# Four transformer stages on one NeuronCore: a batch loop ahead of the token steps, or a quarter of the next batch in each of them

## The chip, the cores and the metric

One core of one Trainium2 chip runs the whole program. The metric is the device time in microseconds of one execution, as the median of several runs; a profiled execution of the same program gives the trace.

## The reference

The input x is 4 batches of 512 tokens of 512 values. Four residual stages follow each other, each on the layer norm of what came before:

```python
x = x + tanh(g_xattn[0]) * smooth_quant_mlp(ln(x), fside, ctx)     # A: two int8 "SmoothQuant" linears, silu between
x = x + tanh(g_ffn[0])   * bit_ffn(ln(x), gate_w, val_w, out_w)    # B: ternary weights, 512 -> 2048 -> 512
x = x + tanh(g_xattn[1]) * (ln(x) @ attention(ctx).T)              # C: softmax((ctx Wq+bq)(ctx Wk+bk).T), 512 x 512 a batch
x = x + tanh(g_ffn[1])   * moe(ln(x), router_w, down_w, up_w)      # D/E: 8 experts, top 2

def smooth_quant_linear(x, w):
    s = sqrt(max|x| over tokens / max|w| over rows)                # one value a column
    x_q, w_q = round((x / s) / x_scale), round((w * s) / w_scale)  # a scale for each row
    return x_q @ w_q.T * x_scale * w_scale.T
```

Stage A needs all 512 tokens of a batch for its column maxima: its first linear (called h) has a 512 x 512 weight, its second (called o) a 512 x 256 weight, and both weights differ in every batch. Stage C's attention weights depend on the batch's context alone. B, C, D and E work on 128 tokens at a time.

## The kernel before

The instructions of each engine are written out by hand in one program order, and engines meet through counting semaphores. An engine takes its instructions strictly in that order, so one that waits holds everything behind it. There are two blocks.

The first block (L377 to L1306) handles whole batches. `step0` loads the ternary weights of gate and val, rounds and transposes them, and does the first linear of batch 0 and the column maxima of batch 1. Then a hardware loop, `step(b)` for b = 1 and 2 and once more for 3, does the first linear of batch b, the second linear and the attention weights of batch b-1, and the column maxima of batch b+1. The attention weights of all four batches stay in `att_t`. `last_step(3)` does the second linear and attention of batch 3 and, between them, sums, rounds and transposes the out weights (`w_sum`, `w_round`, `w_ternary`, `w_transposed` with m = 2).

The parts of a batch are, on PE: `columns` (fp32 transposes for the column maxima), `rows` (spreads the smoothing factors over the partitions by a product with ones), `integers` (fp16 transposes of the rounded values), `scale_row`, `products`, and for attention `t_context`, `t_query_key`, `t_energies`, `t_transpose`. ACT copies what PE leaves in PSUM, rounds to integers (`rounded`, four activations) and exponentiates. DVE takes maxima, scales and dequantises; POOL takes roots, makes diagonals and scales the weights and the hidden values by rows.

The second block (L1344 to L1692) has 16 token steps of 128 tokens. In step i PE computes four chunks of gate and val (`b_chunk`, L1618 to L1625, each a bias product and four products for each of the two), the output of step i-1 (`b_output`, 16 products on activations that 4 DMA transposes deliver), the transpose and the attention product of step i-1 (`spread` of `ln_c`, `c_attend`), and router, experts and their output of steps i-2 and i-3. A chunk's gate goes through ACT (silu), its val through DVE (product with the silu, then the maximum). `p_gate` and `p_val` have two PSUM banks each, `p_tr` and `p_out` two each. ACT's order in a step is: silu 0, norms, silu 1, `lt_d`, silu 2, `ln_c`, rounding of x, `lt_c`, silu 3, copy of x, four roundings.

## Time and profile before

| | us |
|---|---|
| median of 3 runs (598.85 to 600.71) | 600.53 |
| the profiled execution | 600.03 |
| its span, first to last instruction | 598.2 |
| PE busy in the span | 467.9 |
| DVE busy | 417.7 |
| ACT busy | 332.4 |
| POOL busy | 220.2 |

The mean TensorE clock granted is 0.922 of full speed. Engines: PE is TensorE's matmul, DVE VectorE, ACT ScalarE, POOL GpSimd, SP the engine that issues the DMAs. A timeline row gives start and duration in us, then engine, line, operation, output<-input and count, and in brackets the idle time ahead of it with what ended it. A group row gives total busy time and the mean in ns after the bar.

### The profile page before, as it was taken

Reading aid. Unit: us, or ns where it says so; the run is one execution under the profiler, and the core shown is the slowest. Engines: PE = TensorE matmul, PEld = TensorE weight load, DVE = VectorE, ACT = ScalarE, POOL = GpSimd, SP = SyncE. Lnnn points to the kernel's source line nnn. Section 1 sums busy time; section 2 is a strip of 40 time slices with the busy share of each in tenths; the row PEclk is TensorE's granted clock in tenths of the full one; section 3 lists DMA queues with packets and bytes.
Section 4 is the critical chain, followed back from the end, with each engine's and each line's share of the span. In section 5 each row is a group of like instructions: output and inputs, shape, how many; then the busy total and the mean of one; then the engine's idle time right before and its main releaser. Section 6 shows DMA issues by size and latency. Waiting matters only on the chain.

```text
span 598.2 us, 7373 instructions
## 1 busy us (share of the span) xinstructions
PE 467.9 (78%) x2278; PEld 240.1 (40%) x2310; DVE 417.7 (70%) x983; ACT 332.4 (56%) x543; POOL 220.2 (37%) x343
## 2 busy tenths in 40 slices
PE   0546867857865657689899999999999998999863
PEld 0425544434433334233344444444444444444332
DVE  4678798998994687455576677667766776576541
ACT  2558769829838839654545555555555455554411
POOL 2344255535535345522333333333333342332121
PEclk9865999979978987799999999999999999999995
DMA  8985003021003500010121022102220122022210
GB/s 315 249 334 176 1 5 107 1 70 35 0 1 116 200 1 18 1 35 1 36 37 35 19 53 54 35 21 51 54 51 13 44 54 38 19 50 54 36 38 32
DMA packets 56547, 37.25 MB, mean 62 GB/s; under 512 B 43192, under 2 KB 45496, under 8 KB 56000
## 3 DMA queue, kind: packets, MB, share of 16 engines
q1 hardware_dynamic: 56512, 36.82, 21.5%
q8 instruction: 17, 0.28, 0.2%
q14 instruction: 18, 0.15, 0.1%
HBM read 24.15 MB, written 4.19 MB: 47 GB/s over the span
## 4 chain that ended last, share of the span: by engine, by line
PE 44%; issue 4%; ACT 4%; DMA 3%; SPq 2%; DVE 1%; POOLq 0%; POOL 0%
PE p_gate L1625 9%; PE p_out L1632 8%; PE p_out L1665 7%; PE p_val L1625 7%; DMA p_t<-p 3%; PE p_gate L1622 3%; PE p_tr L1613 3%; PE p_out L1650 2%; PE p_out L1640 2%; ACT ln_c L214 2%; SPq L1356 2%; ACT p L1561 1%; PE p_out L1654 1%; PE p_tr L252 1%; PE p_out L1661 0%
## 5 line engine op out<-in xcount | busy, mean ns | idle before, releaser
L1556 ACT ACTIVATE silu_g<-p_gate,bcol 128x512 f32<-128x512 f32 x64 | 44.0, 687 | 97.3 <-PE p_gate L1625 83.2
L1412 DVE TENSOR_TENSOR u<-p_val,silu_g 128x512 f32<-128x512 f32 x64 | 44.3, 692 | 44.2 <-PE p_val L1625 44.2
L1625 PE MATMUL p_val<-val_t,q_room 128*128 128x512 bf16 x256 | 67.0, 385 | 0.0
L1665 PE MATMUL p_out<-out_t,p_t 128*128 128x512 f16 x256 | 61.0, 385 | 6.3 <-DMA p_t<-p 6.3
L1625 PE MATMUL p_gate<-gate_t,q_room 128*128 128x512 bf16 x232 | 61.6, 384 | 4.0 <-issue 4.0
L1381 POOL TENSOR_TENSOR ey<-e_base,y 128x8 f32<-128x8 f32 x16 | 26.5, 1657 | 99.0 <-DVE y L1452 99.0
L1632 PE MATMUL p_out<-att_t,lt_c 128*128 128x512 f32 x128 | 58.4, 599 | 0.7 <-ACT lt_c L1529 0.7
L164 POOL TENSOR_TENSOR rstd<-mv,ln_eps 128x1 f32<-128x1 f32 x48 | 9.2, 193 | 118.9 <-DVE mv L209 118.8
L1428 DVE SCALAR_TENSOR_TENSOR x_all<-p_out,tanh_g,x_all 128x512 f32<-128x512 f32 x32 | 24.0, 750 | 38.0 <-PE p_out L1632 25.2
L1561 ACT ACTIVATE p<-u,bcol 128x512 f16<-128x512 f32 x64 | 40.9, 709 | 10.3 <-DVE bcol L1422 10.3
L1414 DVE TENSOR_REDUCE mu<-u 128x1 f32<-128x512 f32 x64 | 43.9, 686 | 2.2
L1665 PEld LDWEIGHTS p_out<-out_t,p_t 128*128 128x128 f16 x256 | 23.7, 99 | 41.4 <-DMA p_t<-p 15.2
L1625 PEld LDWEIGHTS p_val<-val_t,q_room 128*128 128x128 bf16 x256 | 25.3, 99 | 30.8 <-issue 1.1
L207 DVE BATCH_NORM_STATS2 stats<-x_all 128x6 f32<-128x512 f32 x48 | 32.7, 681 | 3.4 <-PEq L377 2.0
L920 ACT ACTIVATE q_room<-out_t,qscale 128x512 f16<-128x512 f32 x32 | 20.4, 713 | 24.2 <-DVE qscale L668 24.2
L1632 PEld LDWEIGHTS p_out<-att_t,lt_c 128*128 128x128 f32 x128 | 23.1, 190 | 23.9 <-issue 23.0
L1625 PEld LDWEIGHTS p_gate<-gate_t,q_room 128*128 128x128 bf16 x256 | 19.9, 98 | 30.2 <-issue 15.3
L518 POOL TENSOR_TENSOR x_all<-x_all,o_hs 128x512 f32 (+1 forms) x16 | 20.5, 1306 | 22.3 <-DVE o_hs L677 22.3
L1622 PE MATMUL p_gate<-bias_rows,q_room 9*128 9x512 bf16 x64 | 24.8, 388 | 4.8 <-PEq L377 3.0
L165 POOL TENSOR_TENSOR rstd<-rstd,half_neg 128x1 f32<-128x1 f32 x48 | 26.3, 549 | 3.8
L632 DVE TENSOR_REDUCE colmax<-p_tr 128x1 f32<-128x512 f32 x32 | 20.9, 686 | 8.4 <-PE p_tr L1114 8.4
L1622 PE MATMUL p_val<-bias_rows,q_room 9*128 9x512 bf16 x64 | 24.9, 388 | 0.0
(225 smaller groups left out, 1063.1 us busy)
## 6 DMA issues: line engine op xcount, KB each, us to landing
att_t<-in_L_ffn_gate_w SPq DMA_DIRECT2D x4, 1024.0 KB, 11.4
h_region<-in_fside_BxS2xS SPq DMA_DIRECT2D x4, 1024.0 KB, 5.5
att_t<-in_L_ffn_val_w SPq DMA_DIRECT2D x4, 1024.0 KB, 9.7
out_dram<-x_all SPq DMA_DIRECT2D x16, 256.0 KB, 2.3
h_region<-in_L_ffn_out_w SPq DMA_DIRECT2D x3, 1024.0 KB, 5.6
x_all<-in_x SPq DMA_DIRECT2D x2, 1024.0 KB, 5.6
ctx_sb<-in_ctx SPq DMA_DIRECT2D x4, 512.0 KB, 3.4
x_all<-in_x SPq DMA_DIRECT2D x1, 2048.0 KB, 10.4
```

Of the source, the lines that this page charges most:

```text
L165: link(nc.gpsimd.tensor_tensor(rstd[:, s:s + 1], rstd[:, s:s + 1], half_neg[:, 0:1], ALU.pow))
L207: link(nc.vector.bn_stats(stats[:, s, :], tile_of(n)))
L1381: nc.gpsimd.tensor_tensor(ey[:, :], e_base[:, :], y[:, :], ALU.pow).then_inc(d_exp, 1)
L1412: nc.vector.tensor_tensor(cols, p_val[:, c % 2, :], silu_g[:, c % 2, :], ALU.mult).then_inc(u_done, 1)
L1414: return nc.vector.tensor_reduce(mu4[:, c:c + 1], cols, AX_X, ALU.max, apply_absolute_value=True)
L1428: nc.vector.scalar_tensor_tensor(tile_of(n), p_out[:, bank, :], factor, tile_of(n), ALU.mult, ALU.add).then_inc(done, 1)
L1556: nc.scalar.activation(silu_g[:, c % 2, :], p_gate[:, c % 2, :], ACT.Silu, scale=col(CG)).then_inc(silu_done, 1)
L1561: nc.scalar.activation(p16[:, cols], u[:, cols], ACT.Copy, bias=ROUND16, scale=col(QS)).then_inc(b_p16, 1)
L1622: nc.tensor.matmul(bank[:, c % 2, :], x_t[n % 2][rows, D:AUG], bias_aug[m][:, cols], start=True, stop=False)
L1625: last = nc.tensor.matmul(bank[:, c % 2, :], x_t[n % 2][:, k * P:(k + 1) * P], w_t[m][:, k, cols], start=False, stop=k == KD - 1)
L1632: last = nc.tensor.matmul(p_out[:, 0, :], lt_c[:, k * P:(k + 1) * P], att_t[:, bass.ds((n // T) * (KD * S) + k * S, S)], start=k == 0, sto ...
L1665: last = nc.tensor.matmul(p_out[:, 0, :], p_t[:, k * P:(k + 1) * P], w_t[2][:, k, :], start=False, stop=k == KH - 1)
```

## The change

The two blocks become one and the batch loop goes. Batch 0 is done ahead of the token steps (`weights_and_first_linear`, `first_batch`: the former `step0` and `last_step`, now with b = 0), and so are the column maxima and first scaling of batch 1. The rest of batches 1 to 3 is cut into quarters, one for each token step: `quarter(i)` gives batch and quarter, so that steps 0 to 2 carry quarters 1 to 3 of batch 1, steps 3 to 6 batch 2, steps 7 to 10 batch 3, and step 11 the leftovers. Quarter 0 is the norm of the batch and its column maxima (and the end of the batch before), 1 context, query and key and the first rounding, 2 the first linear with the first two energies, 3 the second linear with the last two.

PSUM is shared anew: gate and val take turns in a ring of three banks, the fourth (`p_sum`) collects the output and the attention product, `p_tr` serves norms, router and experts, and `p_out` is left to the quarters. `att_t` holds two batches. The out weights are loaded behind the bias rows on SP's queue. The norm of batches 2 and 3 goes from DVE to ACT, the softmax scaling in steps from ACT to POOL; DVE reads the smoothing row from PSUM and not from a copy.

```diff
+        ring = [p_gate[:, 0, :], p_gate[:, 1, :], p_val[:, 0, :]]
+        p_sum = p_val[:, 1, :]
...
+        def half(n, c, m):
+            return ring[(2 * (HC * n + c) + m) % 3]
...
+        def quarter(i):
+            b, k = divmod(i + 5, 4)
+            return b, k, b < NB
...
+                    x_load(2)
+                    sp.wait_ge(bias_split, 2)
...
+                                sp.dma_start(bias_aug[m][row:row + 1, :].rearrange("o (p n) -> o p n", p=P),
+                                             bias_part[:, s, col:col + n]).then_inc(aug_loaded, 16)
+                    for c in range(4):
+                        w16_by(sp, 4 + c)
+                        w_load(2, c)
...
+                def first_batch():
+                    t_context(0)
+                    w_sum(2, 1)
+                    t_query_key(0)
+                    o_smooth_rows(0)
+                    t_exponential(0, 0)
...
                 def step(i):
+                    b, k, live = quarter(i)
                     act.wait_ge(q_cols, i + 1)
                     b_gate(i, 0)
                     if i >= 2:
                         d_norm(i - 2)
+                    if k == 0 and 2 <= b <= NB:
+                        t_transposed(b - 1, 2)
+                        t_transposed(b - 1, 3)
+                    if live and k == 0:
+                        h_normalise(b)
+                    if live and k == 1:
+                        t_context(b)
+                    if live and k == 2:
+                        t_exponential(b, 0)
+                        t_exponential(b, 1)
+                        h_rounded(b, 1)
+                    if live and k == 3:
+                        t_transposed(b, 0)
+                        t_transposed(b, 1)
+                        o_smooth_rows(b)
...
                     b_gate(i, 2)
+                    if live and k == 3:
+                        o_rounded(b, 0)
+                        t_exponential(b, 2)
+                        t_exponential(b, 3)
+                    if live and k == 2:
+                        h_silu(b, 0)
                     if i >= 1:
-                        c_norm(i - 1)
+                        c_transposed(i - 1)
                     if i + 1 < NT:
-                        q_scaled(act, i + 1)
-                    if i >= 1:
-                        c_transposed(i - 1)
+                        q_scaled(i + 1)
+                    if live and k == 1:
+                        h_rounded(b, 0)
                     b_gate(i, 3)
...
+                def half_free(j):
+                    if j >= 3:
+                        pe.wait_ge((silu_done, u_done)[(j - 3) % 2], (j - 3) // 2 + 1)
...
+                def d_project(n):
+                    pe.wait_ge(d_lt, n + 1)
+                    if n + 1 < NT - 1:
+                        pe.wait_ge(c_lt, n + 2)
```

ACT's queue, from the third silu of a step to the silu of the tokens in D: before, in any step (`q_room` holds x, `p` the rounded activations, `lt_c` the transposed norm).

```order
L1556 ACTIVATE silu_g<-p_gate,bcol 128x512
L214 ACTIVATE ln_c<-x_all,shift,rstd 128x512
L240 ACTIVATE q_room<-q_room,bcol 128x512
L1529 ACTIVATE lt_c<-p_tr 128x512
L1556 ACTIVATE silu_g<-p_gate,bcol 128x512
L244 ACTIVATE q_room<-p_tr 128x512
L245 ACTIVATE q_room<-p_tr 128x128
L1561 ACTIVATE p<-u,bcol 128x512 x4
L1551 ACTIVATE silu_h<-p_out 128x128
```

The same stretch in step 2, which carries quarter 3 of batch 1 (`norm_room` is now `lt_c`, `x` the rounded x, `p_room` the rounded activations, `a_f` the hidden values, `act_f` takes their integers).

```order
L1215 ACTIVATE silu_g<-p_val,bcol 128x512
L1131 ACTIVATE act_f<-a_f,qscale 128x256 x4
L1165 ACT_TABLE_LOAD
L1165 ACTIVATE e_att,z_att<-p_out,neg_max 128x512 x2
L1063 ACTIVATE norm_room<-p_tr 128x512
L1191 ACTIVATE x<-ln_b,bcol 128x512
L1215 ACT_TABLE_LOAD
L1215 ACTIVATE silu_g<-p_gate,bcol 128x512
L1131 ACTIVATE act_f<-ctx_sb,qscale 128x256 x4
L1195 ACTIVATE x_t<-p_tr 128x512
L1196 ACTIVATE x_t<-p_tr 128x128
L1220 ACTIVATE p_room<-u,bcol 128x512 x4
```

Rounding, a table load and two exponentials have come between the third silu and the copy of `lt_c`, and a second table load and another rounding stand around the fourth silu; `ln_c` has moved ahead of the third silu.

SP's queue at the end of the weight loads, as it is now (before, the 18 bias rows were followed by the loop's loads of `fside` and `ctx`, and the out weights were loaded in its last pass, into other rooms).

```order
L305 DMA w_in<-in_fside_BxS2xS_0 128x4x512
L308 DMA ctx_sb<-in_ctx 128x4x256
L302 DMA x_all<-in_x 128x4x512
L357 DMA bias_rows<-bias_part 1x128x16 x18
L311 DMA u<-in_L_ffn_out_w 128x2048
L311 DMA p_room<-in_L_ffn_out_w 128x2048
L311 DMA norm_room<-in_L_ffn_out_w 128x2048
L311 DMA att_t<-in_L_ffn_out_w 128x2048
```

The four loads of the out weights stand behind the bias rows.

PE's queue in the step that carries quarter 2 of a batch, from the output product to the first product of the first linear.

```order
L1560 MATMUL p_out<-qk_t 128x512 x2
L1602 MATMUL p_val<-out_sums,neg_offset 128x512
L1606 MATMUL p_val<-out_t,p_room 128x512 x16
L1477 MATMUL p_out<-ident,q_room 128x128 x16
L1582 MATMUL p_val<-bias_rows,x_t 128x512
L1582 MATMUL p_gate<-bias_rows,x_t 128x512
L1585 MATMUL p_val<-gate_t,x_t 128x512 x4
L1585 MATMUL p_gate<-val_t,x_t 128x512 x4
L1632 MATMUL p_tr<-ident,norm_room 128x128 x4
L1648 MATMUL p_tr<-ident,a_d 128x128
L1497 MATMUL p_out<-h_diag,ones 128x512
L1516 MATMUL p_out<-act_f 128x512 x4
```

And the same place before:

```order
L1661 MATMUL p_out<-out_sums,neg_offset 128x512
L1665 MATMUL p_out<-out_t,p_t 128x512 x16
L1622 MATMUL p_gate<-bias_rows,q_room 128x512
L1622 MATMUL p_val<-bias_rows,q_room 128x512
L1625 MATMUL p_gate<-gate_t,q_room 128x512 x4
L1625 MATMUL p_val<-val_t,q_room 128x512 x4
```

The energies stand ahead of the output product, 16 fp16 transposes of the batch's rounded weights between it and the next chunk, and the scale row and first product behind that chunk.

## Rows read from the trace of the kernel before

**Rows 1.** Busy time by stage: window, us, each engine's busy us, clock, DMA
```profile
80.56:204.10 123.54, 86.09 (x452) 50.45 (x457) 102.69 (x168) 89.65 (x157) 58.84 (x38) 0.92 0.16 51
204.10:248.50 44.40, 27.01 (x151) 16.07 (x151) 33.09 (x55) 29.55 (x46) 26.51 (x26) 0.82 0.11 45
344.44:364.12 19.68, 18.75 (x89) 8.81 (x91) 14.08 (x42) 10.53 (x19) 6.81 (x16) 1.00 0.17 41
```

**Rows 2.** Timeline of PE: the context transposes of batches 0 and 3, the first token step
```profile
80.56 1.09 PE L1172 MATMUL p_val<-ident,ctx_sb 128*128 128x128 f32 x8 [1.62 <-ACT val_t L874]
...
204.10 1.05 PE L1172 MATMUL p_val<-ident,ctx_sb 128*128 128x128 f32 x8
...
248.48 0.58 PE L1622 MATMUL p_gate<-bias_rows,q_room 9*128 9x512 bf16 x1 [2.96 <-PEq L377]
```

**Rows 3.** Timeline of PE in token step 5: its start, and its transposes of the norm
```profile
344.44 0.39 PE L1622 MATMUL p_gate<-bias_rows,q_room 9*128 9x512 bf16 x1
...
355.82 0.66 PE L1613 MATMUL p_tr<-ident,ln_c 128*128 128x128 f32 x4 [0.61 <-ACT ln_c L214]
```

**Rows 4.** SP's issue of the bias rows, the landing of loads, ACT's sum, PE's energies
```profile
77.84 11.54 SPq L425 DMA_DIRECT2D bias_rows<-bias_part  x18
...
h_region<-in_L_ffn_out_w SPq DMA_DIRECT2D x3, 1024.0 KB, 5.6
q_room<-in_L_ffn_out_w SPq DMA_DIRECT2D x1, 1024.0 KB, 7.7
...
206.99 1.91 ACT L887 ACTIVATE h_side<-q_room 128x2048 f16<-128x2048 f32 x1
...
214.36 1.98 PE L1187 MATMUL p_val<-qk_t 128*128 128x512 f32 x4 [0.78 <-ACT qk_t L944]
```

**Rows 5.** Timeline of PE: query and key, rows, bf16 products, fp32 transposes
```profile
82.40 3.70 PE L1179 MATMUL p_val<-ctx_t,wqk_t 128*128 128x512 f32 x8
...
111.63 1.03 PE L1162 MATMUL p_gate<-h_region 128*128 128x512 bf16 x4
...
113.54 1.04 PE L1194 MATMUL p_val<-ident,e_att 128*128 128x128 f32 x8
114.41 1.88 PE L1123 MATMUL p_tr<-h_region,ones 128*128 128x512 f32 x4
```

**Rows 6.** Timeline of ACT: rounding, copies of integers, table load, exponential
```profile
130.61 2.56 ACT L920 ACTIVATE q_room<-out_t,qscale 128x512 f16<-128x512 f32 x4 [11.89 <-DVE qscale L668]
...
136.66 3.74 ACT L874 ACTIVATE h_region<-p_tr 128x1024 bf16<-128x1024 f16 x4
...
140.91 1.28 ACT L948 ACT_TABLE_LOAD   x1
142.20 0.69 ACT L948 ACTIVATE e_att<-p_val,neg_max 128x512 f32<-128x512 f32 x1
```

**Rows 7.** A small DVE instruction beside POOL's, POOL's scaling, and group means
```profile
226.38 1.52 DVE L667 TENSOR_SCALAR scale<-rowmax 128x4 f32<-128x4 f32 x1
...
225.90 1.98 POOL L470 TENSOR_SCALAR h_region<-q_room,inv_gamma_w 128x2048 f16<-128x2048 f32 x1 [3.33 <-issue]
...
140.97 2.37 POOL L511 TENSOR_TENSOR a_f<-a_f,o_rows 128x1024 f32<-128x1024 f32 x1 [1.36 <-ACT o_rows L870]
...
L1412 DVE TENSOR_TENSOR u<-p_val,silu_g 128x512 f32<-128x512 f32 x64 | 44.3, 692 | 44.2 <-PE p_val L1625 44.2
...
L1428 DVE SCALAR_TENSOR_TENSOR x_all<-p_out,tanh_g,x_all 128x512 f32<-128x512 f32 x32 | 24.0, 750 | 38.0 <-PE p_out L1632 25.2
...
L518 POOL TENSOR_TENSOR x_all<-x_all,o_hs 128x512 f32 (+1 forms) x16 | 20.5, 1306 | 22.3 <-DVE o_hs L677 22.3
...
L165 POOL TENSOR_TENSOR rstd<-rstd,half_neg 128x1 f32<-128x1 f32 x48 | 26.3, 549 | 3.8
```

**Rows 8.** Busy time in two windows of the old tail, the clock third from the right
```profile
217.00:222.00 5.00, 0.56 (x3) 0.30 (x2) 4.96 (x5) 3.33 (x6) 4.08 (x2) 0.99 0.00 0
222.00:226.00 4.00, 1.97 (x8) 1.57 (x8) 3.86 (x9) 2.26 (x2) 0.67 (x2) 0.50 0.01 4
```

More of the change, by code:

```diff
@@ L1621, in b_chunk @@
                         rows = slice(m * BIAS_AT, m * BIAS_AT + SPLITS * SPLITS)
[L1622 to L1623 removed]
+                        nc.tensor.matmul(half(n, c, m), x_t[n % 2][rows, D:AUG], bias_aug[m][:, cols], start=True, stop=False)
+                    for m, done in enumerate((gate_mm, val_mm)):
                         for k in range(KD):
[L1625 removed]
+                            last = nc.tensor.matmul(half(n, c, m), x_t[n % 2][:, k * P:(k + 1) * P], w_t[m][:, k, cols],
```

2279 lines of the change are left out of this document (1188 added, 1091 removed).

## The prediction

> **What bounds the kernel now.** I read the busy time by stage first. The reader is to see three unlike stretches [rows 1]. The batch stage (80.56 to 204.10) has DVE as its fullest engine, 102.7 of 123.5 us; the first attention of the tail (204.10 to 248.50) has no full engine and a TensorE clock of 0.82; a token step takes 19.68 us with PE busy 18.75 of it, DVE 14.1, ACT 10.5 and POOL 6.8. So the token steps are bound by PE, and DVE has 5.6 us to spare in each. The timeline of PE gives the stage's edges: the transposes of the context of batch 0 begin at 80.56, those of batch 3 at 204.10, and the first token step at 248.48 [rows 2]. Inside a step PE hardly waits: its only gap of note is 0.61 us for `ln_c` [rows 3].
>
> **What the change removes.** The three passes of the batch loop between those two context transposes go: 204.10 - 80.56 = 123.5 us. What follows them (last_step) stays, now for batch 0 (first_batch).
>
> **What it puts in their place, first term: a late load.** last_step sums the third weight matrix while it does its attention: ACT did so at 206.99, 2.9 us after the context transposes, and the energies came at 214.36, 10.3 us after them [rows 4]. The loads had been issued long before. Now SP issues them behind the 18 bias DMAs, which run from 77.84 for 11.5 us [rows 4], so from 89.4. One such 1 MB load lands 5.6 us after its issue, and the one issued right behind another after 7.7 [rows 4]; for each further one I take 3 us. Chunk 1 then lands at about 98, ACT's sum of it (1.9 us) stands ahead of the query and key copies on ACT's queue, and the energies can start at about 101.5: 20.9 us after the context transposes in place of 10.3. The stretch starts **10.7 us** late, and DVE, which sums chunks 2 and 3 after its first maxima, finds them landed. If the loads share the queue better, it is 7 us; if they come later one by one, 13.
>
> So the token steps start at 248.5 - 123.5 + 10.7 = 135.7, a gain of **112.8 us**. The barrier between the two blocks goes as well, but the first token's statistics now wait for the additions to x; I count these as even.
>
> **Second term: PE's work in the steps.** Prices on PE, from [rows 5]: 0.9 us for 8 fp32 transposes (also for 16 fp16 ones, which I estimate from the same spacing), 0.88 for an fp32 product of 512 columns, 0.22 for a bf16 one. The quarters are: 1 (context transposes 0.9, smoothing rows 1.8, query and key 3.5, half the integers 0.9) 7.1; 2 (two energies 1.7, integers 0.9, scale row 0.9, 16 products 3.5, transposes of the hidden values 0.9) 8.0; 3 (softmax transposes 0.9, rows 0.9, two energies 1.7, integers 0.9, scale row 0.9, products 0.9) 6.2; 0 (32 transposes 3.7, the rest of the previous batch 1.8) 5.5. That is 26.7 us a batch, and 19.4 for batch 1, whose quarter 0 and rows are done ahead: 19.4 + 2 x 26.7 + 1.8 of leftovers in step 11 = **74.5 us**. If nothing else waited, the span would be 598.2 - 112.8 + 74.5 - 3 = 557 us.
>
> **Third term: what PE waits for.** The other engines' work rides along, and I walked each quarter in program order, every engine starting an item when its own queue and its inputs allow. Times below count from the first matmul of the step.
>
> Quarter 3 is the worst. DVE reduces the hidden values' columns (to 0.9), takes the ratio, adds and takes statistics (3.1); POOL's root waits behind its other root (5.1), and DVE's product waits for it (6.95). d_gate, the addition and two statistics (11.5) follow. POOL does two roots, three instructions each, 1.1 to 1.3 us with the power's 0.55 in it (13.05), and two scalings of 2.37 us (15.4, 17.75) [rows 7]. DVE's row scale ends in a 4-column instruction, and such a one sat out a POOL instruction: 1.52 us, ending just after POOL's own end, where its neighbour of the same kind takes about 0.2 [rows 7]. So ACT gets its scale at 18.15, rounds four tiles to 19.85, loads the Exp table (1.28) and exponentiates twice (22.6) [rows 6]. Behind that on ACT stand the copy `lt_c` (23.1), which PE's d_project now waits for because it shares the bank, the rounding of x (23.7), the load of the Silu table (25.0), the last silu (25.7) and the rounding of the context (27.3). PE is free at 17.75 and waits 5.4 us; free again at 24.85 it waits 2.5 for the integers, then attends to 31.4, and its scale row waits for ACT, which has the step's four roundings first (30.6), and for POOL's diagonal (32.65). The quarter ends at **34.9**, where PE alone would need 25.2.
>
> Quarter 2: ACT is 2.75 us late from quarter 1's integers, does silu and norm (6.65), the Exp load and two exponentials (9.55), and only then the rounding of the weights, 2.5 us [rows 6] (12.05), which PE has wanted since 7.6. Two copies of integers, 0.93 us each [rows 6], keep PE's products waiting to 17.1, and the transposes of the hidden values wait at the end for a silu behind ACT's roundings (31.6). It ends at **32.5** against 27.0.
>
> Quarter 0: DVE's second pair of dequantised tiles waits for POOL's additions, 1.31 us each [rows 7], behind a root and the deviation (8.25), and PE's softmax transposes for DVE (1.5); the normalisation, now four activations on ACT (to 13.0), holds its first transposes 1.1: **27.0** against 24.5. Quarter 1: DVE's scaling reads PSUM and I give it 2.3 us, the length of its undisturbed form; **26.8** against 26.2.
>
> Together 121.2 us for four steps that took 78.7: +42.5 a batch, as much as one pass of the old loop took (41.2). Twice that is 85. Batch 1 has quarters 1 to 3 only, three quarters of 42.5 less 3 because step 0 starts with no work carried in: 29. With 2 for the leftovers in step 11 it is **116 us**.
>
> **Fourth term: the clock.** After PE's gap in the old tail, the granted clock was 0.50 from 222 to 226, and eight transposes took 1.97 us where they take 1.04 [rows 5, 8]. Half speed is the 1.2 GHz level. The gaps of 4.5 us in quarter 2 and 5.4 in quarter 3 are of that length. I charge 1.5 us to each, some of it hidden behind ACT: **+8 us**.
>
> **Fifth: plain steps.** c_norm moves ahead of the third silu, which takes away the 0.61 us gap of the last four steps [rows 3]; with a shorter prologue (no copy of the first row) I take 3.3 us off.
>
> **Sum.** 598.2 - 112.8 + 116 + 8 - 3.3 = 606.1 us of span. The profiled run took 1.8 us more than its span, 600.03, and stands 0.5 below the median of 600.53. The forecast is **608 us**.
>
> What could move it: DVE's products (0.69) and additions (0.75) [rows 7] leave little doubt. POOL's softmax scaling has no row; between a quarter of its 1.98 us instruction on 2048 columns (0.5, taken, as the same kind of operation) and an addition (1.31) nothing changes, as c_norm has 2.7 us of slack there. Were DVE's scaling disturbed by POOL as in the old loop, it could cost 4 us in each of two steps. The walk itself may be wrong by 4 us a batch.
>
> The Exp and Silu tables alternate twice in quarter 2 and twice in quarter 3. In the trace the load takes 1.28 us and the exponential starts 0.01 us after its end [rows 6]. The Trainium skill (ScalarE: Activation LUTs, section What ACT_TABLE_LOAD costs) adds a drain of 1.38 us to each switch, 2.66 in all; the trace shows none, so the measurement decides, and by the page the sum would be about 12 us higher.
>
> **The rivals.** (A) *The waits are shorter than walked, and PE stays the bound*: ACT and POOL would have to run ahead of PE, so that the roundings of quarters 2 and 3 are there when asked for. For it: DVE, the fullest helper, would have 14.1 + 34.2/4 = 22.7 us of work in a step of 26 (34.2 is a third of the batch stage's 102.7 [rows 1]). Against it: both stalls rest on an order written out by hand. Half the waits and no clock loss give 585 us; it decides once the two stalls of quarter 3 (7.9 us) come to under 4. (B) *ACT is the bound of quarters 2 and 3*: each table switch costs another 1.28 us in its place, nine of them on the path, 12 us, and PE runs at half clock through the rest of these steps, another 6: 625 us. (C) *The late load does no harm*, since chunk 1 lands before ACT asks: 596 us.
>
> **How the numbers follow.** Forecast as walked 0.50, A 0.30, B 0.14, C 0.06. A difference of 0.3%, 1.8 us, is about what a measurement of this kernel can tell. Faster by more: A's 0.27 and 0.06 of the rest, 0.33; within: 0.12; slower by more: 0.55. The forecast's own range is 596 to 619; leaving out PE-bound ends of A below 580 and B's above 628 makes 580 to 628.
>
> **What would show it.** Token steps begin near 136; steps of quarter 3 last 33 to 36 us, of 2 31 to 34, of 0 and 1 26 to 28, plain ones 19.1; ACT's sum of `out_w` waits for its load from 82 to 98; PE's longest gap in a live step stands before `router_down_t`, released by the copy of `lt_c`. Live steps of under 28 us on average would prove me wrong in the third term, an energy before 95 us in the first.

## The result and the profile after

The changed kernel takes 612.41 us (median of 4 runs, 609.53 to 613.07), the kernel before 599.74 beside it: a ratio of 1.0202, 95% interval 1.0163 to 1.0241. It is **2% slower**; 608 was forecast. The profiled execution has a span of 610.8 us against 598.2.

First the windows by stage, with the columns of [rows 1]: from the context transposes of batch 0 to the first token step, the twelve steps that carry or finish quarters, and the rest.

```profile
78.81:134.65 55.84, 26.89 (x148) 16.14 (x150) 30.65 (x50) 29.45 (x46) 24.85 (x22) 0.75 0.31 110
134.65:495.24 360.59, 311.34 (x1456) 157.20 (x1480) 248.39 (x621) 211.98 (x362) 152.18 (x237) 0.93 0.13 31
495.24:610.80 115.56, 94.96 (x408) 44.17 (x413) 67.83 (x206) 45.63 (x81) 30.66 (x67) 0.93 0.17 41
```

Three differences make up the 12.6 us of span. The token steps begin at 134.65 in place of 248.48 [rows 2], 113.8 earlier. Steps 0 to 11 take 360.6 us; the same twelve took 234.2 before (248.48 to 482.68), so they grew by 126.4. From step 12 to the end nothing changes: 115.56 against 115.5. The balance is 126.4 - 113.8 = 12.6.

| step of batch 2, batch 3 | forecast, with its share of the clock term | measured |
|---|---|---|
| quarter 0 (steps 3, 7) | 27.0 | 27.4, 27.4 |
| quarter 1 (4, 8) | 26.8 | 27.1, 27.1 |
| quarter 2 (5, 9) | 32.5 + 1.5 | 33.0, 33.9 |
| quarter 3 (6, 10) | 34.9 + 1.5 | 37.9, 38.0 |
| leftovers (11) | 21.7 | 22.9 |
| plain (12, 13, 14) | 19.1 | 20.2, 19.9, 20.8 |

The waits of PE over the whole run (who waited for whom: us in total, times, the longest) name the places that matter in the steps, beside the one of the late load in the first batch:

```profile
PE p_tr L1640 <- ACT norm_room L1063: 14.6, 4, 4.9
PE p_val L1560 <- ACT qk_t L1161: 14.3, 1, 14.3
...
PE p_out L1477 <- ACT q_room L1122: 10.4, 4, 4.0
...
PE p_out L1502 <- POOL o_diag L458: 7.1, 3, 3.2
```

L1640 is `d_project`, which waits for the copy of `lt_c` (the copies have one line, L1063); L1560 the energies; L1477 the integers of quarter 2; L1502 the scale row of quarter 3.

**The late load.** Timelines of SP, ACT and PE answer to [rows 4]:

```profile
76.00 11.49 SPq L357 DMA_DIRECT2D bias_rows<-bias_part  x18
...
95.45 1.91 ACT L1080 ACTIVATE silu_g<-p_room 128x2048 f16<-128x2048 f32 x1 [14.83 <-DMA p_room<-in_L_ffn_out_w]
...
98.66 3.78 PE L1560 MATMUL p_val<-qk_t 128*128 128x512 f32 x4 [14.29 <-ACT qk_t L1161]
```

ACT stands idle for 14.83 us for chunk 1, with the copies of query and key behind it, and the energies come 19.85 us after the context transposes (78.81) in place of 10.3. Behind that gap the four products of the energies take 3.78 us, where they took 1.98 before [rows 4].

**Quarter 3.** PE in step 6, which begins at 308.06 and ends at 345.96, and POOL in the same stretch:

```profile
330.88 2.15 PE L1640 MATMUL p_tr<-router_down_t,norm_room 128*128 128x136 f32 x8 [4.88 <-ACT norm_room L1063]
...
334.99 0.82 PE L1490 MATMUL p_out<-ident,act_f 128*128 128x128 f16 x8 [0.57 <-ACT act_f L1131]
335.64 3.65 PE L1624 MATMUL p_val<-att_t,norm_room 128*128 128x512 f32 x8
342.43 2.08 PE L1502 MATMUL p_out<-o_diag,ones 128*128 128x512 f32 x2 [3.14 <-POOL o_diag L458]
344.73 1.29 PE L1523 MATMUL p_out<-act_f 128*128 128x512 bf16 x3 [0.22 <-issue]
```

```profile
336.61 3.11 POOL L483 TENSOR_SCALAR e_att<-e_att,rz_att 128x512 f32<-128x512 f32 x2 [8.62 <-DVE rz_att L752]
339.70 1.67 POOL L527 TENSOR_TENSOR ey<-e_base,y 128x8 f32<-128x8 f32 x1
341.34 1.04 POOL L458 TENSOR_TENSOR o_diag<-ident,gated_scale 128x512 f32<-128x512 f32 x1
```

PE's router product begins 22.8 us into the step (the walk had 23.15) and its attention product ends at 31.2 (walk: 31.4). That the second time fits is in part luck: the wait for the integers is 0.57 us where the walk had 2.5, and the router's eight products behind the gap take 2.15 us (1.17 in E2, at full clock). Only then do the two part. The diagonal was forecast at 32.65 and ends at 34.3, because POOL does two softmax scalings and a power ahead of it. The scaling takes 1.57 us where 0.5 had been taken. The scale row then runs at half speed, 2.08 us for two, where two such take 1.10 at full clock (E3 shows it below).

**Quarter 2.** PE in step 5 (from 275.04), and the clock behind its gap (window, us, busy time of PE, PEld, DVE, ACT, POOL, the clock, DMA share, GB/s):

```profile
286.62 1.07 PE L1477 MATMUL p_out<-ident,q_room 128*128 128x128 f16 x16 [3.98 <-ACT q_room L1122]
287.62 0.61 PE L1582 MATMUL p_gate<-bias_rows,x_t 9*128 9x512 bf16 x2
288.16 1.46 PE L1585 MATMUL p_gate<-gate_t,x_t 128*128 128x512 bf16 x3
289.84 1.64 PE L1585 MATMUL p_gate<-val_t,x_t 128*128 128x512 bf16 x4 [0.22 <-issue]
```

```profile
287.60:291.20 3.60, 3.38 (x11) 1.24 (x11) 0.00 (x0) 1.38 (x3) 3.35 (x7) 0.53 0.00 0
292.80:296.20 3.40, 3.40 (x19) 1.61 (x18) 2.10 (x6) 3.19 (x7) 0.70 (x4) 1.00 0.02 5
```

The integers start 11.6 us into the step (walk: 12.05). Behind the gap the granted clock is 0.53, the 1.2 GHz level, and the same two groups take 1.46 and 1.64 us in place of 0.81 and 1.03: 1.3 us lost, where 1.5 was charged.

### The profile page after: what moved, and what is told of

Read it like the earlier page. It is cut to its first block and busy times, and to the rows that moved or that the text cites. A ratio compares the mean times of both kernels' runs of the same rounds, so it can differ in the third digit from the quotient of the medians.

```text
span 610.8 us, 7320 instructions
## 1 busy us (share of the span) xinstructions
PE 474.3 (78%) x2277; PEld 247.2 (40%) x2310; DVE 404.2 (66%) x975; ACT 332.0 (54%) x541; POOL 237.4 (39%) x363
## 5 line engine op out<-in xcount | busy, mean ns | idle before, releaser
L1624 PE MATMUL p_val<-att_t,norm_room 128*128 128x512 f32 x128 | 62.0, 630 | 0.7 <-ACT norm_room L1063 0.7
L1606 PE MATMUL p_val<-out_t,p_room 128*128 128x512 f16 x256 | 59.0, 379 | 2.9 <-DMA p_room<-p_room 2.7
L1215 ACT ACTIVATE silu_g<-p_gate,bcol 128x512 f32<-128x512 f32 x43 | 29.5, 686 | 50.6 <-PE p_gate L1585 37.3
L804 DVE TENSOR_TENSOR u<-p_gate,silu_g 128x512 f32<-128x512 f32 x43 | 29.6, 688 | 41.0 <-PE p_gate L1585 28.7
L1176 ACT ACTIVATE norm_room<-x_all,shift,rstd 128x512 f32<-128x512 f32 x32 | 26.1, 814 | 42.9 <-POOL shift L491 42.7
L1220 ACT ACTIVATE p_room<-u,bcol 128x512 f16<-128x512 f32 x64 | 40.9, 710 | 13.5 <-DVE bcol L814 13.5
L1585 PE MATMUL p_gate<-val_t,x_t 128*128 128x512 bf16 x168 | 45.7, 393 | 0.6 <-issue 0.4
L1585 PE MATMUL p_gate<-gate_t,x_t 128*128 128x512 bf16 x159 | 43.5, 394 | 2.1 <-issue 1.8
L1606 PEld LDWEIGHTS p_val<-out_t,p_room 128*128 128x128 f16 x256 | 24.4, 98 | 34.8 <-DMA p_room<-p_room 6.7
L1624 PEld LDWEIGHTS p_val<-att_t,norm_room 128*128 128x128 f32 x128 | 24.8, 202 | 26.8 <-issue 25.4
L1640 PE MATMUL p_tr<-router_down_t,norm_room 128*128 128x136 f32 x128 | 21.7, 322 | 14.6 <-ACT norm_room L1063 14.6
L1215 ACT ACTIVATE silu_g<-p_val,bcol 128x512 f32<-128x512 f32 x21 | 14.4, 686 | 27.0 <-PE p_val L1585 17.6
L490 POOL TENSOR_TENSOR rstd<-rstd,half_neg 128x1 f32<-128x1 f32 x48 | 26.3, 548 | 3.7
L1640 PEld LDWEIGHTS p_tr<-router_down_t,norm_room 128*128 128x128 f32 x128 | 20.3, 225 | 18.3 <-issue 15.5
L1582 PE MATMUL p_gate<-bias_rows,x_t 9*128 9x512 bf16 x86 | 25.5, 399 | 0.9 <-ACT x_t L1196 0.9
## 6 DMA issues: line engine op xcount, KB each, us to landing
norm_room<-in_L_ffn_gate_w SPq DMA_DIRECT2D x1, 1024.0 KB, 12.3
```

What stands on the lines that cost most here:

```text
L490: link(nc.gpsimd.tensor_tensor(rstd[:, s:s + 1], rstd[:, s:s + 1], half_neg[:, 0:1], ALU.pow))
L804: nc.vector.tensor_tensor(cols, half(n, c, 1), silu_g[:, c % 2, :], ALU.mult).then_inc(u_done, 1)
L1176: nc.scalar.activation(dst[:, :], tile_of(n), ACT.Identity, bias=shift[:, s:s + 1], scale=rstd[:, s:s + 1]).then_inc(done, 1)
L1215: nc.scalar.activation(silu_g[:, c % 2, :], half(n, c, 0), ACT.Silu, scale=col(CG)).then_inc(silu_done, 1)
L1220: nc.scalar.activation(p16[:, cols], u[:, cols], ACT.Copy, bias=ROUND16, scale=col(QS)).then_inc(b_p16, 1)
L1585: last = nc.tensor.matmul(half(n, c, m), x_t[n % 2][:, k * P:(k + 1) * P], w_t[m][:, k, cols], start=False, stop=k == KD - 1)
```

## The experiments

The table sums them up. The last column is against the 612.4 us of the changed kernel; each ratio is to the kernel before, timed beside it.

| | edit to the changed kernel | us | ratio, 95% interval | us against 612.4 |
|---|---|---|---|---|
| E1 | loads ahead of the bias DMAs | 597.66 | 0.9974, 0.9952 to 0.9996 | -14.8 |
| E2 | quarter 3: exponentials behind `lt_c` | 610.43 | 1.0170, 1.0136 to 1.0205 | -2.0 |
| E3 | quarter 3: diagonal ahead of the scalings | 603.83 | 1.0055, 1.0031 to 1.0078 | -8.6 |
| E4 | own bank for `ln_c` in plain steps | 612.93 | 1.0213, 1.0181 to 1.0245 | +0.5 |
| E5 | quarter 2: roundings first | 611.49 | 1.0210, 1.0158 to 1.0261 | -0.9 |
| E6 | no Exp in the softmax | 600.09 | 1.0030, 0.9997 to 1.0064 | -12.3 |
| E7 | E2 and E3 | 606.13 | 1.0121, 1.0070 to 1.0173 | -6.3 |
| E8 | E1, E2, E3 and E5 | 589.32 | 0.9840, 0.9790 to 0.9891 | -23.1 |
| E9 | softmax scalings on DVE | 600.73 | 1.0031, 1.0012 to 1.0051 | -11.7 |
| E10 | E1, E3, E5, POOL's scalings last in quarter 2 | 583.15 | 0.9719, 0.9680 to 0.9758 | -29.3 |
| E11 | E10, quarter 3 rearranged | 575.56 | 0.9599, 0.9568 to 0.9630 | -36.9 |
| E12 | E11, scale row earlier, own bank | 568.11 | 0.9464, 0.9433 to 0.9496 | -44.3 |

The ratios of E2, E4 and E5 lie inside the interval of the changed kernel (1.0163 to 1.0241), so these three differences cannot be told from none.

The profiled executions also differ where no edit reaches. Below, the same four products behind the same gap, in the changed kernel and in E1, and then E1's attention products in step 6, which E1 leaves as it is:

```profile
74.22 1.98 PE L1452 MATMUL p_tr<-h_diag,ones 128*128 128x512 f32 x4 [2.85 <-POOL h_diag L446]
```

```profile
74.30 3.78 PE L1452 MATMUL p_tr<-h_diag,ones 128*128 128x512 f32 x4 [2.86 <-POOL h_diag L446]
...
322.39 5.47 PE L1624 MATMUL p_val<-att_t,norm_room 128*128 128x512 f32 x8
```

The granted clock from 74 to 78 us is 1.00 in the one and 0.50 in the other. The attention products took 3.65 us in the changed kernel's step 6. Step 6 as a whole takes 37.9 us there and 36.7 in E1, step 0 takes 21.2 and 19.8. So a single step can be over 1 us longer or shorter without any edit, by how long TensorE stays at its lower clock, and the lengths of single steps are to be read with that in mind.

### E1: the loads ahead of the bias DMAs

```diff
                     x_load(2)
+                    for c in range(4):
+                        w16_by(sp, 4 + c)
+                        w_load(2, c)
                     sp.wait_ge(bias_split, 2)
...
-                    for c in range(4):
-                        w16_by(sp, 4 + c)
-                        w_load(2, c)
```

> The loads of the out weights go ahead of the 18 bias DMAs on SP's queue. Theory (first term of the prediction, as the trace after gives it): the late load costs 9.6 us, 19.85 us from the context transposes to the energies in place of 10.26, so the first token step begins near 125 in place of 134.65 and the time is 603. Rival 1 (the load does no harm, another wait stands behind it): 612. Rival 2: the bias DMAs, now later, hold the first chunk of gate and val: about 608.

597.66 us, 14.8 less, more than the 9.6 expected, 0.3% below the kernel before. SP now issues the last load at 61.64, and PE's timeline reads:

```profile
81.05 1.06 PE L1537 MATMUL p_val<-ident,ctx_sb 128*128 128x128 f32 x8 [1.27 <-ACT val_t L1067]
...
87.39 1.98 PE L1560 MATMUL p_val<-qk_t 128*128 128x512 f32 x4 [0.78 <-ACT qk_t L1161]
...
121.34 0.61 PE L1582 MATMUL p_gate<-bias_rows,x_t 9*128 9x512 bf16 x2 [0.95 <-ACT x_t L1196]
```

The energies come 6.3 us after the context transposes, 13.5 less than in the changed kernel, where the expectation had 9.6. The 10.3 us of the old tail, from which both it and the prediction had counted, held two delays that the first batch does not have. In the trace of before the transposes of the hidden values waited 2.21 us for dequantised tiles of the batch before, and query and key, at a low clock, took 5.29 us against 3.70:

```profile
207.36 1.13 PE L1114 MATMUL p_out<-ident,a_f 128*128 128x128 f32 x8 [2.21 <-DVE o_hs L677]
208.29 5.29 PE L1179 MATMUL p_val<-ctx_t,wqk_t 128*128 128x512 f32 x8
```

2.2 + 1.6 = 3.8 us, so the wait alone costs 13.5. From the energies to the first token step another 2.0 us go (35.99 against 33.95), 1.8 of them in the energies themselves, at half clock behind the long gap (3.78 against 1.98). Together that is 15.5 us, near the 14.8 of the medians. The token steps begin only 13.3 us earlier in this trace because the context transposes came 2.2 us later, behind the slow products at 74.30. Both rivals of this run fell: no other wait stands behind the load, and the bias rows are in time.

### E2: the exponentials behind lt_c

```diff
                     if live and k == 3:
                         o_rounded(b, 0)
-                        t_exponential(b, 2)
-                        t_exponential(b, 3)
...
                         q_scaled(i + 1)
+                    if live and k == 3:
+                        t_exponential(b, 2)
+                        t_exponential(b, 3)
```

> Only ACT's order in quarter 3 changes: the two exponentials stand behind the copy lt_c and the rounding of x. Theory: PE's gap ahead of router_down_t (4.1, 4.9, 4.9 us) is the Exp load and the exponentials that stand ahead of lt_c, about 2.8 us of them; it falls to about 2, and a part comes back as a wait for the integers, which now come later: 2 us gained in each of three steps, 606. Rival: everything comes back at the integers, since ACT has the same work ahead of them: 612.

610.43 us, which cannot be told from 612.4. The waits of PE over the run show where the gain went (all line numbers behind the edit are one higher):

```profile
PE p_out L1491 <- ACT act_f L1131: 9.9, 3, 3.6
...
PE p_tr L1641 <- ACT norm_room L1063: 6.3, 4, 2.1
...
PE p_out L1491 <- ACT e_att L1165: 3.4, 3, 1.3
```

The wait for `lt_c` falls from 14.6 to 6.3, and at the integers, three instructions later on PE, the wait for the roundings is 9.9 where there was 0.57 in a step, with another 3.4 for the exponentials. The rival was right: ACT has the same work ahead of the integers whichever way it is ordered. And the quarter ends with another wait, which this edit leaves alone. POOL's diagonal and PE's scale row in step 6, which begins at 308.20:

```profile
341.47 1.04 POOL L458 TENSOR_TENSOR o_diag<-ident,gated_scale 128x512 f32<-128x512 f32 x1
```

```profile
342.57 1.12 PE L1503 MATMUL p_out<-o_diag,ones 128*128 128x512 f32 x2 [1.16 <-POOL o_diag L458]
```

The diagonal is ready 34.3 us into the step and the scale row begins at 34.4, both as in the changed kernel. That the step ends at 36.7 and not 37.9 is no gain of the edit: E1's step 6, which does not have it, takes 36.7 too.

### E3: the diagonal ahead of the softmax scalings

```diff
                     if live and k == 3:
-                        t_normalise(b, 2)
-                        t_normalise(b, 3)
+                        scale_diagonal(1, b)
                     if i >= 2:
                         softmax_power(i - 2)
+                    if live and k == 3:
+                        t_normalise(b, 2)
+                        t_normalise(b, 3)
```

> Only POOL's order at the end of quarter 3 changes: scale_diagonal and softmax_power stand ahead of the two softmax scalings. Theory: PE's wait for o_diag (3.1 us, with 3.1 us of scalings and 1.7 of power ahead of it on POOL) goes wholly, because its input gated_scale was there 11 us before; with a little of the clock that falls after the gap 3 to 4 us in each of three steps: 602. Rival: the scaled softmax, now later, holds its transposes in the next step, 1.5 us more there: 607. Second rival: PE waits at the same place for ACT's copies of the integers (p_out), which end at 340.3: half of the gap stays, 607.

603.83 us, 8.6 less, near the theory's 602; both rivals (607) fell. POOL and PE in step 6:

```profile
330.66 1.04 POOL L458 TENSOR_TENSOR o_diag<-ident,gated_scale 128x512 f32<-128x512 f32 x1 [2.78 <-DVE gated_scale L719]
336.17 1.65 POOL L527 TENSOR_TENSOR ey<-e_base,y 128x8 f32<-128x8 f32 x1 [4.47 <-DVE y L845]
337.82 3.12 POOL L483 TENSOR_SCALAR e_att<-e_att,rz_att 128x512 f32<-128x512 f32 x2
```

```profile
339.44 1.10 PE L1502 MATMUL p_out<-o_diag,ones 128*128 128x512 f32 x2
```

The diagonal is there 7.7 us before PE asks; PE's gap of 3.14 us is gone and with it the half clock (1.10 us in place of 2.08). Steps 6 and 10 take 33.8 and 33.9 us in place of 37.9 and 38.0. The later scalings do not hold the next step: PE's wait in quarter 0, for DVE, stays at 1.57.

### E4: a bank of its own for ln_c, first try

```diff
-            return p_tr[:, 0, :] if n + 1 < NT else p_gate[:, 0, :]
+            return (p_tr[:, 0, :] if n < 11 else p_out[:, 0, :]) if n + 1 < NT else p_gate[:, 0, :]
```

> From step 12 on the transposes of ln_c go into p_out's first bank and not into the one that they share with ln_d. Theory: the 0.83 us gap ahead of them in plain steps (copy of lt_d not done) goes, 0.8 in each of three or four steps: 609.5. Rival: plain steps are bound by the round trip of the four DMA transposes (gaps of 0.7 and 1.1 at the 13th product), the gap moves there: 612.

612.93 us, no difference, and the trace has the gap where it was, on the new bank:

```profile
508.94 0.63 PE L1618 MATMUL p_out<-ident,norm_room 128*128 128x128 f32 x4 [0.83 <-ACT norm_room L1063]
```

This run shows nothing on either theory. The wait for the copy of `lt_d`, which guards the shared bank, is an instruction of its own in `c_spread` and was left in. E12 mends it.

### E5: the roundings of quarter 2 first

```diff
+                    if live and k == 2:
+                        h_rounded(b, 1)
                     act.wait_ge(q_cols, i + 1)
                     b_gate(i, 0)
...
                         t_exponential(b, 1)
-                        h_rounded(b, 1)
```

> Only ACT's order in quarter 2 changes: the four roundings of the weight (2.55 us) stand at the head of the step, ahead of silu 0, and no longer between the exponentials and silu 1. Theory: PE's gap of 4.0 us ahead of the transposes of these integers falls to about 2, since ACT had 2.2 us of idle time ahead of the norm, and with the gap goes the stretch at half clock behind it (1.3 us): 2 to 3.3 us in each of three steps, 603 to 606. Rival: the exponentials alone end as late as before (Exp load, two exponentials, behind a later silu), the gap stays over 3.5: 611.

611.49 us: within what the measurement tells apart. The gap did shrink as the theory had it, from 3.98 to 1.29, but its gain was lost behind it. PE in step 5:

```profile
284.37 1.27 PE L1478 MATMUL p_out<-ident,q_room 128*128 128x128 f16 x16 [1.29 <-ACT e_att L1165]
...
295.30 0.63 PE L1619 MATMUL p_tr<-ident,norm_room 128*128 128x128 f32 x4 [2.47 <-ACT norm_room L1063]
```

and ACT ahead of that copy:

```profile
292.77 0.81 ACT L1176 ACTIVATE norm_room<-x_all,shift,rstd 128x512 f32<-128x512 f32 x1 [3.29 <-POOL shift L491]
```

ACT now idles 3.29 us for POOL's root of the token's norm, which stands behind POOL's two softmax scalings. This is the slack that the prediction had put at 2.7 us: it was slack only as long as ACT itself was late.

### E6: no table switch

```diff
-                        nc.scalar.activation(e_att[:, t % 2, :], t_bank[b][:, t % 2, :], ACT.Exp, bias=neg_max[:, t:t + 1],
+                        nc.scalar.activation(e_att[:, t % 2, :], t_bank[b][:, t % 2, :], ACT.Silu, bias=neg_max[:, t:t + 1],
```

> The exponentials are computed as silu, so the softmax is not computed, and no table is switched inside a step or in first_batch; every other instruction and wait is the same. Theory: a switch costs its load of 1.28 us and nothing more, of which one load stands in the way of PE in quarter 2 and one or two in quarter 3: 1.3 + 1.3 to 2.6 in each of three batches, with a little of the clock, and 1.3 to 2.6 in first_batch: 600 to 604. Rival (B of the prediction, a switch costs 2.56 or more and ACT is the bound of quarters 2 and 3): 590 or less. Second rival: the gaps are set by other waits, under 3 us in all: 610.

Here the exponential is computed as a silu, so the kernel leaves out the softmax; the run only prices the table loads. 600.09 us, 12.3 less, and 15.1 by the spans of the profiled executions (610.8 and 595.7). These groups of ACT's are in the changed kernel and not in this run:

```profile
L1165 ACT ACT_TABLE_LOAD x7 | 9.0, 1283 | 0.1
L1215 ACT ACT_TABLE_LOAD x6 | 7.7, 1283 | 0.1
L1275 ACT ACT_TABLE_LOAD x1 | 1.3, 1283 | 0.0
```

Fourteen loads are 18.0 us of ACT, and 12.3 to 15.1 come back, 0.9 to 1.1 us a load. That is at the edge of what the theory gave (600 to 604) and far from rival B's 590. It is not a clean price of one load, since part of it is clock: in step 10 the scale row takes 1.12 us again in place of 2.08. That a switch takes no more than its load is read from ACT itself, in step 6 of the changed kernel:

```profile
325.78 1.70 ACT L1131 ACTIVATE act_f<-a_f,qscale 128x256 f16<-128x256 f32 x4 [2.82 <-DVE qscale L716]
327.50 1.28 ACT L1165 ACT_TABLE_LOAD   x1
328.80 0.69 ACT L1165 ACTIVATE e_att<-p_out,neg_max 128x512 f32<-128x512 f32 x1
```

The load starts 0.02 us after the roundings end and the exponential 0.02 us after the load. But much of the loads' time is on the path: quarter 3 falls by 4.0 us in steps 6 and 10, and quarter 2 by 1.4 and 2.0, so the part of rival B that has PE wait for ACT in quarters 2 and 3 holds. The Trainium skill (ScalarE: Activation LUTs, section What ACT_TABLE_LOAD costs) gives 2.66 us for a switch, with a drain; fourteen of these would be 37 us, an estimate from the page's figure, and this run shows no such sum.

### E7 and E8: together

E7 has the edits of E2 and E3, E8 those of E1, E2, E3 and E5.

> Both reorderings of quarter 3 together (exponentials behind lt_c, diagonal ahead of the softmax scalings). Theory: two separate waits, the gains add: 2.0 and 8.6 us, 601.8. Rival: the later exponentials and the diagonal meet (integers copied later, the gap ahead of the scale row is then ACT's), so the sum is no more than the diagonal's alone: 604.

> Early load, exponentials late, diagonal first and roundings first together. Theory: the four costs are separate waits in separate places and add up: 14.8 + 2.0 + 8.6 + 7 (the last as expected for it alone) below 612.4, so 580, 3.3% faster than before. Rival: PE's clock or its own work (85.7 of 121.2 us of a batch were busy) takes part of it back, 587.

E7 takes 606.13 us, no less than E3 alone with 603.83: the edits do not add, and the later exponentials may even take back 2.3 us of what the diagonal gave. PE in step 6 (306.90 to 341.68):

```profile
333.80 0.87 PE L1491 MATMUL p_out<-ident,act_f 128*128 128x128 f16 x8 [3.16 <-ACT act_f L1131]
334.47 5.12 PE L1625 MATMUL p_val<-att_t,norm_room 128*128 128x512 f32 x8
```

The eight attention products take 5.12 us, 3.65 in the changed kernel: the wait has moved to just before them, and the stretch at low clock falls on PE's longest work. This happens without the edit too, but not always. In the traces with ACT's order of the changed kernel (that one, E1, E3, E4, E5, E9 and E10) these products take over 5 us in 10 of 21 quarters 3; with the later exponentials (E2, E7, E8) they take 4.85 to 6.15 in all nine. So where a gap stands seems to matter as well as its length; that this makes up E7's 2.3 us is argued, not shown.

E8 takes 589.32 us, 1.6% faster than the kernel before, 9 us above the theory's 580. The four single gains add to 26.3 us with E5's as measured, and 23.1 came: most of the gap is E5's expected 7, which E5 alone had already missed, and E7 had shown that E2 and E3 give 6.3 together and not 10.6.

### E9: the scalings on DVE

```diff
                     if live and k == 2:
                         t_reciprocal(b, 0)
+                        t_normalise(b, 0)
+                        t_normalise(b, 1)
...
                     if live and k == 3:
                         t_reciprocal(b, 2)
+                        t_normalise(b, 2)
+                        t_normalise(b, 3)
```

and POOL's two calls are left out. DVE already has `t_normalise`.

> One part of the change undone: the softmax scalings in the steps are DVE's again (12 instructions), right behind their reciprocals. Theory: what POOL's scaling costs (1.57 us each in place of the 0.5 that the prediction took) is the wait for o_diag and nothing else of weight, so this gives what the reordering on POOL gave, 8.6 us: 604. Rival 1: the scalings also held c_norm and q_norm back in quarter 2 (POOL does them ahead of those roots), another 1 to 2 us in each of three steps: 599. Rival 2: DVE's extra work delays its product and the ring of banks: 608.

600.73 us, 11.7 less: this one move gives back nearly all of what the change costs and leaves it 0.3% slower than the kernel before. It does not quite undo a part of the change, as its expectation says: in the kernel before ACT did these twelve scalings, 0.72 us each, and DVE those of the last batch only. The page's groups of the scaling, in the changed kernel and in this run (here the four of the first batch are among them):

```profile
L483 POOL TENSOR_SCALAR e_att<-e_att,rz_att 128x512 f32<-128x512 f32 x12 | 18.7, 1570 | 45.9 <-DVE rz_att L752 45.9
```

```profile
L751 DVE TENSOR_SCALAR e_att<-e_att,rz_att 128x512 f32<-128x512 f32 x16 | 9.9, 662 | 0.3
```

The same operation takes 1.57 us on POOL and 0.66 on DVE. Quarter 3 falls to 33.8 and 35.3 us; quarter 2 stays (33.0 and 34.3), so rival 1's mechanism is not what gave the 3.1 us beyond E3. Steps 2, 5, 6, 9 and 10 together are 8.1 us shorter than in the changed kernel, and 7.8 in E3: there the two edits are worth the same. Of the rest 1.3 us is in step 0 (19.9 in place of 21.2), which is as short in E1 and E2, whose edits do not reach it; the remainder lies in small differences of both signs and stays open.

### E10 to E12: the order of quarters 2 and 3, put right step by step

E10 is E1, E3 and E5 with one more edit, on POOL in quarter 2:

```diff
-                    if live and k == 2:
-                        t_normalise(b, 0)
-                        t_normalise(b, 1)
                     if i >= 1:
                         c_root(i - 1)
...
                         softmax_power(i - 2)
+                    if live and k == 2:
+                        t_normalise(b, 0)
+                        t_normalise(b, 1)
```

> Early load and diagonal first, and in quarter 2 the roundings at the head of the step (ACT) and POOL's two scalings behind its roots and its power. Theory: the gain that the roundings alone did not give was lost where PE then waited for lt_d (2.5 us), behind two norms whose roots stood behind POOL's scalings; with both, quarter 2 takes 30 to 31 us in place of 33 to 34: 14.8 + 8.6 + 3 x 2.7 below 612.4, 581. Rival: the gap moves once more (to the integers' copies or the first silu), quarter 2 stays at 33: 589.

583.15 us. Quarter 2 takes 29.5 us, in step 5 and in step 9. E1 and E3 alone add to 23.4, so the pair of edits in quarter 2 gives 5.9, if the gains add; E5 by itself gave 0.9. Quarter 3, with the edit of E3 alone, takes 35.4 and 35.5 us here and 33.8 and 33.9 in E3: its attention products take 5.6 and 5.5 us in place of 3.7. Why they fall at the lower clock in all three batches of this run is open.

E11 rearranges quarter 3 on three engines:

```diff
 # ACT, step
                         o_rounded(b, 0)
-                        t_exponential(b, 2)
-                        t_exponential(b, 3)
...
                     if live and k == 3:
-                        o_rounded(b, 1)
+                        t_exponential(b, 2)
+                        t_exponential(b, 3)
                     if i + 1 < NT:
                         x_transposed(i + 1)
+                    if live and k == 3:
+                        o_integers_transposed(b, 0)
+                        o_integers_transposed(b, 1)
...
                     if live and k == 3:
-                        o_integers_transposed(b, 0)
-                        o_integers_transposed(b, 1)
                         o_scale_row(b)
 # PE, step
-                    if live and k == 3:
-                        o_integers(b, 0)
-                        o_integers(b, 1)
                     if i >= 1:
                         c_attend(i - 1)
...
+                    if live and k == 3:
+                        o_integers(b, 0)
+                        o_integers(b, 1)
 # DVE, step
                         row_scales(1, b, 1)
+                        o_rounded(b, 1)
```

> As the run before, and quarter 3 rearranged: the second four roundings go from ACT to DVE, which idles 2.8 us there; silu 3 stands ahead of the exponentials; c_attend stands ahead of the integers on PE; the integers' copies stand ahead of the four token roundings. Theory: quarter 3 is bound by ACT's chain, which becomes 1.7 us shorter and loses PE's wait for it under c_attend's 3.65 us; quarter 3 falls from 33.8 to about 31: 8 below the run before, 573. Rival: the chain of copy, scale row and product, no longer hidden by c_attend, costs what is gained: 581.

(DVE also gets a definition of `o_rounded`, four scalings of 256 columns.) 575.56 us, 7.6 less, where 8 was expected; quarter 3 falls from 35.4 and 35.5 us to 34.2 and 33.1, not to 31. The rival is half right, and names the next wait, which is the largest left in a step:

```profile
PE p_out L1534 <- ACT o_rows L1073: 11.7, 4, 3.8
```

ACT copies the scale row behind four token roundings and a table load. E12 puts it ahead of them and mends E4:

```diff
 # ACT, step
                         o_integers_transposed(b, 1)
+                        o_scale_row(b)
                     act.wait_ge(b_qs, i + 1)
...
-                    if live and k == 3:
-                        o_scale_row(b)
 # PE, c_spread, with the bank of E4
-                    need(pe, d_lt, n)
+                    if n < 11 or n + 1 == NT:
+                        need(pe, d_lt, n)
```

> As the run before, with two edits in separate places. In quarter 3 ACT's copy of the scale row stands ahead of the four token roundings (the new 3.8 us wait of PE's second product was for it). From step 12 on the transposes of ln_c go into p_out's bank and their wait for the copy lt_d goes too (in the earlier run with this bank the wait had been left in, so it could show nothing). Theory: quarter 3 loses 2.5 to 3 us in each of three batches, a part of it given back where the token's DMA transposes now come later; the 0.84 us gap ahead of the transposes of ln_c in steps 12 to 14 goes, and these steps fall from 20.2 to 19.4: 575.6 - 8 - 2.4 = 565. Rivals: the later roundings cost as much at the next output as the row gives, 573; plain steps keep their length, since the products wait for their DMA transposes, and the bank gives under 1.

568.11 us: **5.4% faster than the kernel before** and 7.2% faster than the change. PE's second product waits 0.26 us for the scale row:

```profile
314.82 0.60 PE L1533 MATMUL p_out<-act_f 128*128 128x512 bf16 x2 [0.26 <-ACT o_rows L1073]
```

Steps 6 and 10 take 30.7 and 29.1 us; most of the difference between the two is again the attention products, 5.35 and 3.65 us. The bank gave little, as its rival had it: the gap at `ln_c` is gone from the plain steps, and 0.47 us comes back at the next instruction, which now waits for ACT's copy of `a_dt`:

```profile
484.89 1.12 PE L1663 MATMUL p_tr<-up_t,a_dt 128*128 128x512 f32 x2 [0.47 <-ACT a_dt L1073]
```

Steps 12 to 14 take 20.3, 19.6 and 19.6 us, 20.5, 19.9 and 19.9 in E11.

## Why the prediction was right, and where it was not

608 us, slower, was forecast, and 612.41 came. By spans it is 606.1 against 610.8, and the terms stand like this:

- **The late load: right, by two errors that cancel, which is luck.** The start of the token steps was forecast at 135.7 and came at 134.65, a gain of 113.8 us where 112.8 was taken. ACT waited from 80.6 to 95.45, where 82 to 98 was expected. But the 10.3 us taken over from the old tail held 3.8 us of delays of its own. Without the late load the token steps begin 127.1 us earlier than before, not 123.5, and the load takes 13.3 of that in the traces, not 10.7 (15.5 with the start of the stretch lined up, E1). No clock was charged behind this gap, PE's longest, and it cost 1.8 us. Rival C fell: the load does harm, and removing it is the largest single gain.
- **The live steps: 126.4 us added, 116 and 8 forecast for waits, work and clock together.** The walk had quarters 0 and 1 within 0.4 us and quarter 2 within 1.0. Batch 1's three steps took 85.9 us where the terms give 91 (59 of plain steps, 29, and 3 of the clock). Errors cancel here too: the 29 takes three quarters of a whole batch's 42.5, though the walk's own quarters 1 to 3 add 35.2; and these steps took 55.4 us before the change, not 59. They grew by 30.5.
- **Quarter 3: the mechanism right, one size off.** The wait for `lt_c` was forecast as the longest, 5.4 us, and is 4.88. The step of the prediction that failed is the one that took 0.5 us for POOL's softmax scaling and said that up to 1.31 nothing changes. It takes 1.57, outside the bounds, and the prediction asked only what that does to c_norm in quarter 2. In quarter 3 the two scalings stand ahead of the diagonal on POOL. They make it 1.65 us late, and PE's gap of 3.14 us costs another 1 to 1.5 at half clock. Against the forecast of 36.4 us (with its clock) the quarter took 1.5 us more in step 6 and 1.6 in step 10: this is what the mis-sized scaling cost. E3 puts the price of the whole order on POOL at 8.6 us, a part of which the forecast held already. Without it the change would be 0.6% slower than before, not 2%. The walk's second stall, 2.5 us for the integers, was mis-sized as well: it is 0.57.
- **The clock: right in size.** 1.3 us was lost behind the gap of quarter 2, 1.5 charged. That it fits is no more than a mean: the same products behind the same gap took 1.98 or 3.78 us in two executions.
- **Plain steps: wrong.** 3.3 us were taken off because `ln_c` comes earlier. From step 12 to the end nothing was gained, 115.56 against 115.5. The gap of 0.61 us [rows 3] is one of 0.84, since `ln_c`'s transposes now share a bank with `ln_d`'s and wait for the copy `lt_d` (in E12, without that wait, the gap is gone). The prediction saw the shared bank for `d_project` and overlooked it one place earlier.
- **The rivals.** A (585 us, ACT and POOL ahead of PE) fell: the two stalls of quarter 3 come to 5.5 us, more than the 4 from which it would have decided. Its reasoning returns in E12, where the waits are gone and the same quarters give 568. B is half right (E6): PE waits for ACT in quarters 2 and 3, and removing the loads gives 12.3 to 15.1 us, but a switch costs 1.28 us and no more.

The sum of the misses is 1.0 earlier at the start, 2.4 more in the live steps and 3.3 not gained in the plain ones: 4.7 us, as between 606.1 and 610.8.

## What to carry to other kernels

Work that is laid into the gaps of a loop must be ordered on each helper engine by when its result is asked for: here 44 us of 612 came back, nearly all of it where a needed copy, scale or load had stood behind something that nobody was waiting for yet. Besides the orders, only four roundings in each quarter 3 changed their engine and one tile its bank. After one such wait is removed, look at the same step again before judging it: E5 gave nothing until the POOL order behind it was mended too, and E2 nothing because the diagonal set the end of the quarter. And when an operation moves to an engine that has no row for it, ask what it costs in every place where it will stand, and keep the upper bound at the cost of the slowest like operation, not below it.

## What the hardware showed that was not expected

- One fp32 scaling of 128x512 by a column takes 1.57 us on POOL, more than an addition of two such tiles there (1.31, [rows 7]), and 0.66 on DVE (E9; the four of the first batch in the changed kernel took 1.13 on DVE). On ACT it took 0.72 before.
- TensorE's clock fell to the 1.2 GHz level after gaps of 3 to 5 us, as forecast, but shorter gaps can do it too, and not always. Behind a gap of 2.85 us the same four fp32 products took 1.98, 2.50, 3.62, 3.68 or 3.78 us in different executions of the same stretch (the changed kernel, E6, E5, E4, E1); behind one of 2.11 us the eight router products of step 6 took 1.17 in E2 and 1.91 in E7.
- Behind E7's gap of 3.16 us the granted clock was 0.70 from 334.40 to 339.50, and the attention products took 5.12 us where they take 3.65.
- Fourteen table loads, each 1.28 us, gave 12.3 us by the medians and 15.1 by the spans when they went (E6). ACT idled 0.1 us in all ahead of the seven of L1165 and 0.1 ahead of the six of L1215: nothing beyond the load was seen.
